# Gates of a mixture of experts stored by single-element DMAs instead of turned by TensorE

## What is computed

```python
h = relu(einsum('bi,eio->beo', x, eW1) + eb1)          # 8 experts, 1024 -> 1024
h = relu(einsum('beh,eho->beo', h, eW2) + eb2)         # 1024 -> 512
expert_out = einsum('beh,eho->beo', h, eW3) + eb3      # 512 -> 256
gates = softmax(einsum('bi,tie->bte', x, gW) + gb)     # 2 tasks, over 8 experts
tin = einsum('bte,bed->btd', gates, expert_out)
th = relu(einsum('btd,tdh->bth', tin, tW1) + tb1)      # towers 256 -> 512 -> 256 -> 1
th = relu(einsum('bth,tho->bto', th, tW2) + tb2)
out = sigmoid(einsum('bth,tho->bto', th, tW3) + tb3)
```

## Time and profile before

| | |
|---|---|
| median of three timed runs | 573.57 us (572.89 to 573.98) |
| the profiled execution, its own time | 572.65 us |
| its span, first to last instruction | 570.9 us |
| PE busy | 565.4 us, 99% of the span |
| DVE / ACT / POOL busy | 455.0 / 310.8 / 99.9 us |
| granted TensorE clock | 1.00 throughout |
| DMA | 39774 packets, 86.87 MB, 152 GB/s over the span |

### The profile page before, as it was taken

One profiled execution on the slowest core, in us unless ns is written; L12 is line 12 of the kernel. 1 busy time (PEld: TensorE's weight loads), 2 busy tenths in 40 slices (PEclk: granted clock), 3 DMA queues, 4 the chain that ended last, 5 costly groups with the idle time before them and its releaser, 6 DMA issues.

```text
span 570.9 us, 8541 instructions
## 1 busy us (share of the span) xinstructions
PE 565.4 (99%) x2883; PEld 477.2 (84%) x2883; DVE 455.0 (80%) x576; ACT 310.8 (54%) x422; POOL 99.9 (18%) x106
## 2 busy tenths in 40 slices
PE   8999999999999999999999999999999999999998
PEld 6788888888888888888888888888888888888776
DVE  7998579975997769976899759977699768998493
ACT  3484566535763275724665356632757246654553
POOL 0201311052102411033200521024110332003000
DMA  9818675467726674467644577266644676426100
GB/s 324 227 51 233 155 224 130 156 164 173 170 82 190 174 179 110 147 166 201 175 121 162 149 183 167 89 198 175 173 100 147 165 210 168 118 73 211 47 1 0
DMA packets 39774, 86.87 MB, mean 152 GB/s; under 512 B 3521, under 2 KB 8769, under 8 KB 39762
## 3 DMA queue, kind: packets, MB, share of 16 engines
q1 hardware_dynamic: 29762, 66.50, 35.3%
q0 software_dynamic: 9856, 19.96, 20.1%
q10 hardware_dynamic: 144, 0.26, 0.2%
HBM read 86.68 MB, written 0.04 MB: 152 GB/s over the span
## 4 chain that ended last, share of the span: by engine, by line
PE 91%; DVE 3%; DMA 3%; ACT 1%; issue 1%; ACTq 0%; DVEq 0%
PE psum L493 33%; PE psum L496 17%; PE psum L348 14%; PE psum L349 14%; PE psum L350 14%; DMA w_raw<-eW_pairs 2%; DVE w_lo L1004 1%; DMA scratch<-xT 1%; DVE x_both L1135 0%; DVE t_both L1155 0%; DVE x_both L1133 0%; DVE scratch L1039 0%; ACT w_hi L959 0%; DVE scratch L1149 0%; ACT scratch L994 0%
## 5 line engine op out<-in xcount | busy, mean ns | idle before, releaser
L1004 DVE TENSOR_TENSOR w_lo<-w_raw,w_hi 128x1024 fp32r<-128x1024 f32 (+2 forms) x108 | 138.3, 1282 | 21.1 <-ACT w_hi L788 12.0
L348 PE MATMUL psum<-h_hi,w_hi 128*128 128x512 f32 (+1 forms) x340 | 131.9, 388 | 0.8 <-DVE h_lo L1020 0.8
L349 PE MATMUL psum<-h_lo,w_hi 128*128 128x512 f32 (+1 forms) x340 | 131.7, 387 | 0.0
L350 PE MATMUL psum<-h_hi,w_lo 128*128 128x512 f32 (+1 forms) x340 | 131.6, 387 | 0.0
L493 PE MATMUL psum<-t_both,w_hi 128*128 128x512 f32 x480 | 130.9, 394 | 0.0
L493 PE MATMUL psum<-x_both,w_hi 128*128 128x512 f32 x360 | 98.2, 394 | 0.0
L493 PEld LDWEIGHTS psum<-t_both,w_hi 128*128 128x128 f32 x480 | 82.6, 189 | 11.5
L1409 POOL DMA_DIRECT2D w_raw<-eW_pairs x30 | 25.9, 865 | 341.4 <-DMA w_raw<-eW_pairs 340.8
L1020 DVE SCALAR_TENSOR_TENSOR h_lo<-scratch,h_hi 128x512 fp32r<-128x512 f32 (+1 forms) x66 | 66.9, 1014 | 22.8 <-ACT scratch L851 19.5
L496 PEld LDWEIGHTS psum<-t_both,w_lo 128*128 128x128 f32 x480 | 73.7, 189 | 10.2
L1004 DVE TENSOR_TENSOR w_lo<-scratch,w_hi 128x512 fp32r<-128x512 f32 (+1 forms) x60 | 57.2, 954 | 24.6 <-ACT w_hi L781 24.0
(11 more groups left out here) (100 smaller groups left out, 582.4 us busy)
## 6 DMA issues: line engine op xcount, KB each, us to landing
w_raw<-eW_pairs SPq DMA_DIRECT2D x30, 768.0 KB, 4.2
w_raw<-eW SPq DMA_DIRECT2D x40, 512.0 KB, 4.0
scratch<-eW_pairs SPq DMA_DIRECT2D x30, 256.0 KB, 4.9
w_raw<-eW_pairs SPq DMA_DIRECT2D x30, 256.0 KB, 5.1
w_raw<-eW_pairs POOLq DMA_DIRECT2D x30, 256.0 KB, 5.0
scratch<-eW_pairs POOLq DMA_DIRECT2D x30, 256.0 KB, 6.5
scratch<-gates_dram POOLq DMA_DIRECT2D x8, 512.0 KB, 5.6
w_raw<-tW SPq DMA_DIRECT2D x4, 512.0 KB, 4.3
```

What stands on the lines that cost most here:

```text
L348: pe.matmul(bank, weights_hi, moving_hi, start=first, stop=False)
L349: pe.matmul(bank, weights_hi, moving_lo, start=False, stop=False)
L350: return pe.matmul(bank, weights_lo, moving_hi, start=False, stop=last)
L1004: dve.tensor_tensor(wide(w_lo, slots), raw, wide(w_hi, slots).bitcast(F32), ALU.subtract).then_inc(slot_ready, 1)
```

## The change

The transposes that turn the gates back, their copy out of PSUM and POOL's two stores are taken out. In their place SP writes `gate` to `gates_dram` straight from its layout: eight DMAs, one for each block of the batch and each task, each of 128 partitions by 8 experts, where the eight experts of a partition lie side by side in `gate` but 4 KB apart in DRAM, so that the DMA has no run of contiguous bytes longer than one element of 4 bytes. SP issues them after `load_w2(0, 3)` and before `load_blocks(1, 1)`, behind a wait for DVE's last softmax instruction. `turn_logits` moves from ahead of P1 of `pair(0, 3)` to behind P5. POOL waits for eight stores in place of two.

```diff
@@ the sync engine
             sp.wait_ge(slot_ready, split(0, "W2", 1))
             load_w2(0, 3)
+
+            sp.wait_ge(gated_ready, 1)
+            for t in range(T):
+                for b in range(BT):
+                    sp.dma_start(gates_dram[:, t, b * P:(b + 1) * P].rearrange("e p -> p e"), gate[:, b * T + t, :],
+                                 allow_slow_non_contiguous=True).then_inc(gates_stored, DMA)
             for e in range(1, E):
@@ pair
                 product(e, "P5", i)
+                if first and i == PAIRS - 1:
+                    turn_logits()
@@ layer2
                         last_product(e, PAIRS - 1)
-                        turn_gates()
@@ the tensor engine
-            def turn_gates():
-
-                pe.wait_ge(upper_done, nth(0, 2) + 1)
-                pe.wait_ge(gates_ready, 1)
-                for b in range(BT):
-                    mm = pe.transpose(banks[BANK_GATES][0:T * E, b * P:(b + 1) * P],
-                                      gate[:].rearrange("p (b t) e -> p b (t e)", b=BT)[:, b, :], ident[:])
-                mm.then_inc(gates_turned, 1)
-
             pair(0, 2)
-            turn_logits()
             pair(0, 3)
@@ the vector engine
             dve.tensor_tensor(gate[:], gate[:], red[:, 2, :].unsqueeze(2).broadcast_to(wide_gate),
-                              ALU.mult).then_inc(gates_ready, 1)
+                              ALU.mult).then_inc(gated_ready, 1)
 
             upper_fold(0, 3)
             lower_fold(0, 3)
             w2_lo(0, 2)
-            dve.wait_ge(gates_turned, 1)
-            dve.tensor_copy(turned[0:T * E, :], banks[BANK_GATES][0:T * E, :]).then_inc(gated_ready, 1)
             c21_fold(0, 3)
@@ the pool engine
-            pool.wait_ge(gated_ready, 1)
-            for t in range(T):
-                pool.dma_start(gates_dram[:, t, :], turned[t * E:(t + 1) * E, :]).then_inc(gates_stored, DMA)
-            pool.wait_ge(gates_stored, T * DMA)
+            pool.wait_ge(gates_stored, BT * T * DMA)
```

More of the change, by code:

```diff
@@ L102 @@
 BANK_OUT3 = [0, 1]
-BANK_LOGITS, BANK_TURNED, BANK_GATES = 5, 7, 0
+BANK_LOGITS, BANK_TURNED = 5, 7
 BANK_TOWER1 = [[2, 3, 5, 6], [7, 4, 0, 1]]
@@ L295, in moe_towers @@
         exp_done = sem("exp_done")
-        gates_ready = sem("gates_ready")
-        gates_turned = sem("gates_turned")
         gates_stored = sem("gates_stored")
```

## The result

The changed kernel takes 604.5 us (median of six executions, 598.3 to 615.2) where the kernel before takes 573.5. The ratio is 1.0506, with a 95% interval of 1.0476 to 1.0537: 5% or 29 us slower, some 18 us above the top of the forecast range. The four executions that count scatter by 7.2 us, those of before by 1.7. The profiled execution took 605.49 us with a span of 603.7, 32.8 us more than before.

The account below looks back on a forecast made before the run. The prediction took PE, busy 565.4 of 570.9 us, as the bound; 0.44 us of removed transposes and 0.45 of removed wait, with the stores covered, gave 573.57 - 0.89 = 572.7 us, range 572.0 to 584.5.

Parts of the forecast that it names:

- PE's part: On PE, 0.44 us from the gates' transposes removed and 0.45 from the wait before the logits' transposes: 0.89 us gained.
- the moved part: Moving the logits' transposes by three products removes PE's wait before them, so P1 of pair 3 starts 0.45 us earlier.
- Rival C: PE's gain doesn't arrive, P3 or P7 of pair 3 waiting instead: 573.1 to 573.6 us, chance 0.09.
- Rival B: Single-element packets hold SP's queue, expert 1's blocks come late, PE waits at P3 of pair 0: 575.3 to 593.7 us, chance 0.47.
- its opposite: The forecast itself: the eight stores hide while the DMA engines stand idle; 572.7 us, chance 0.44.
- the price of an element: Time that one 4-byte element of the stores holds a DMA engine, taken as 9 to 17 ns.
- the lower of two rows: Lower bound for an element's cost: POOL's packets of next to no bytes, 8.6 ns each; the upper was 57.7 ns.
- The count of 520: Packets of the eight stores for each of 16 DMA engines: 512 runs of 4 bytes and eight completions.
- the prediction's own formula: Change in time once the stores outlast their cover: 520 times an element's cost, less 9.9 us of cover, slack and gain.
- the sum: PE's gain of 0.89 us with everything added elsewhere under cover: 573.57 - 0.89 = 572.7 us.
- The Trainium skill's rule: A plain DMA transposing by strides is 19 times slower than the DMA transpose: 24 ns an element, 2.5 us slower.
- The load behind the stores: Expert 1's blocks, next in SP's queue, with 5.0 us of slack before ACT first uses POOL's sum on them.

Follow-up runs that it names:

- e1: The kernel before with only the logits' transposes moved behind P5 of pair 3: ratio 0.9992, 572.84 against 573.00 us.
- e2: The changed kernel with the gates turned in 32 by 32 blocks by one DVE instruction, stored as 256 runs of 128 bytes: ratio 0.9980, 571.91 against 573.00 us.
- e9: The kernel before plus eight unread single-element stores on SP, elements 32 bytes apart in spare DRAM: ratio 1.0118, 6.8 us slower.
- e7: The kernel before plus eight unread single-element copies on SP into SBUF, elements 32 bytes apart: ratio 1.0020, 1.1 us slower.
- e3: The kernel before, nothing taken out, plus the same eight single-element stores on SP into spare DRAM, elements 4 bytes apart: ratio 1.0561, 32.1 us slower.
- e6: The kernel before plus eight unread single-element stores on SP, elements 512 bytes apart in spare DRAM: ratio 1.0137, 7.9 us slower.
- e10: The kernel before plus eight unread single-element stores on SP, elements 64 bytes apart in spare DRAM: ratio 1.0126, 7.2 us slower.
- e5: The kernel before plus eight unread stores of the same bytes on SP into spare DRAM, as 1024 runs of 32 bytes: ratio 1.0003.
- e11: The kernel before plus two of the eight single-element stores (2048 elements, 4 bytes apart in spare DRAM): ratio 1.0234, 13.4 us slower.
- e8: The changed kernel with the eight single-element stores issued by POOL, between two of its sums, instead of SP: 585.9 and 594.0 us against 573.1.
- e4: The kernel before plus four of the eight single-element stores on SP into spare DRAM, 4 bytes apart: ratio 1.0381, 21.8 us slower.

## Why the prediction was wrong

**PE's part was right, to the hundredth.** It gave 37.4 us for P1, 41.6 for the transposes and 44.85 for P3; the trace has 37.39, 41.60 and 44.84. No row of the gates' transposes is left. e1 puts the moved part at 0.46 us (-0.1 to 1.0) where 0.45 was forecast, and e2, where nothing spoils it, the whole at 1.1 us (0.6 to 1.7) where 0.89 was. Rival C fell. The least difference worth telling was set at 0.2%, and e2 is just there.

**Rival B was what happened**, with a chance of 0.47 given to it as a whole and its place named rightly: SP late, POOL's sum with it, ACT at `g1_hi(1, 1)`, PE at P3 of pair 0. I forecast its opposite, and left 0.13 above 584.5 us, where the time came out. What led there:

**The step that failed is the price of an element, put at 9 to 17 ns, near the lower of two rows.** I bounded it by completions (8.6 ns) and by 1 KB loads (57.7 ns). Neither is a small write of data. The count of 520 for each engine was exact, but the elements took 56 ns each from 57 to 86 us, three to six times what I took and almost the upper row. By the prediction's own formula that makes 520 x 56 ns - 9.9 = 19 us slower, where the sum had 0.89 faster. Nor is the price a constant: it was 10 ns in 57 to 58 us and 73 ns in 60 to 80, it is 21 ns in e9, and 15 ns into SBUF (e7), the only one that my 9 to 17 ns cover. The Trainium skill's rule of the 19 times slower strided DMA ("VectorE: DVE Perf Modes", The three transpose paths), which made 24 ns as an estimate, is near e9's 21 and far from the 56 of the store that the change makes.

**What the sum left out is where the elements land.** Neighbours in DRAM are 4 bytes apart and belong to neighbouring partitions. At 4 bytes the stores cost 32.1 us, at 32 bytes or more 7 to 8 (e3 against e6, e9, e10), and the same bytes in 1024 runs of 32 bytes nothing (e5). So single elements 4 bytes apart hinder each other as those 32 bytes apart don't. The Trainium skill ("DMA: Bandwidth & Descriptors", Specifications) says that below 512 bytes a DMA engine reads, modifies and writes. The runs agree that small writes are dear, but that rule by itself says nothing of the difference between e3 and e9, whose elements are all of 4 bytes; and e5's runs of 32 bytes are below its bound as well and were hidden. Why near ones hinder, in the memory or on the way to it, and whether it takes writes from different DMA engines, no run shows; this stays open.

**The load behind the stores was put at nothing.** I let it begin when they end and then land as fast as ever. Instead the loads stay slow when no element is left in the queue: 25 GB/s in 86 to 91 us, 77 GB/s in e11's 71 to 73, against 292 before. That is 10.6 us of the loss in the changed kernel. With them e9 comes out too: 520 x 21 ns - 9.9 = 1.0 us, and 6.3 us by which its load lands more slowly than 4.2, make 7.3 where 6.8 was measured. It isn't a matter of one queue, for e8 shows 27.2 us for a load in another queue than the stores, and two stores alone add 14.5 us to the landing (e11). SP's own hold at its issues, up to 9.6 us at one where 0.47 us was taken from loads of 128 rows, was not foreseen either. What keeps the loads slow no run shows.

**The clock was left out.** PE's long stop took the granted clock to the 1.2 GHz level, and P3 and P7 cost 2.47 us more behind it, 8% of the profiled execution's 32.8.

## What to carry to other kernels

Don't price a DMA by its bytes, nor its pieces by rows of another kind: for a store of single elements measure one, into a spare array, before building on it; a spare store beside the untouched kernel gave the whole loss here in one run. If a layout has to be turned and only small runs are left, turn it in part first, on an engine that isn't the one waited for, so that each run is longer (32 bytes were free here in e5, 128 in e2): one DVE instruction of 0.24 us made 8192 pieces into 256 and the loss of 29 us into a gain of 1.1. And look at a transfer's cover not only in its own queue, nor only until its last packet: here slow stores held up the loads of the other queue too, and for some 10 us after them.

## What was not expected of the hardware

- Eight single-element DMAs of 1024 elements are issued by SP in 10.4 us with their target in SBUF, in 11.0 us with elements 32 or 512 bytes apart in DRAM, and in 29.6 us at 4 bytes apart; eight of 1024 elements in runs of 32 bytes take 4.3 us.
- Writes to DRAM that are 4 bytes apart also slow the loads behind them, in the same queue or in another: 18.6 and 27.2 us for a load that lands in 4.2; behind those 32 bytes apart it takes 10.5.
- Eight stores of 1024 single elements are 8320 packets when SP issues them and 256 when POOL does, and loads are late behind both.
- Executions with such stores scatter: 598 to 605 us for the changed kernel, 605 to 611 for e3, 589 to 594 for e4, where the kernel before has 572.5 to 574.4.
